# Key products of the second attention layer moved into the expert loop of the first

## The reference

```
# layer 0 mixture: 8 experts, two per token
scores = sigmoid(x @ gate_w.T);  _, sel = top_k(scores + expert_bias, 2)
top = scores at sel
for e in range(8):
    w = sum(where(sel == e, top, 0))
    out = out + square(relu((x * w) @ w_up[e].T)) @ w_down[e].T

# layer 1 attention: 16 heads of 64
q = x @ Wq;  k, v = split(context @ Wkv)
out = softmax(q k^T / 8) v @ Wout + bout
```

## Time and profile before

| | value |
|---|---|
| median of three runs | 838.61 us |
| the profiled execution, its own time | 840.57 us |
| span of the profiled execution | 839.2 us |
| mean granted TensorE clock | 0.952 |
| PE busy, share of the span | 721.9 us, 86% |
| DVE | 531.9 us, 63% |
| ACT | 502.9 us, 60% |
| POOL | 287.6 us, 34% |

### The profile page before, as it was taken

How to read it: one execution, slowest core, us unless ns; L and a number is a source line. 1 busy time by engine, 2 the same in 40 slices (tenths; PEclk the granted TensorE clock), 3 DMA queues, 4 the chain that set the end, 5 groups by cost and what they waited for, 6 DMA issues and landing times.

```text
span 839.2 us, 16594 instructions
## 1 busy us (share of the span) xinstructions
PE 721.9 (86%) x5129; PEld 596.4 (71%) x5129; DVE 531.9 (63%) x1847; ACT 502.9 (60%) x1688; POOL 287.6 (34%) x330
## 2 busy tenths in 40 slices
PE   3999895866787998999998989989999998877597
PEld 2667674656665877787985777878778876666597
DVE  3788674556657887754547888674242056986574
ACT  2988672445558987735556645666544248763375
POOL 1310311635543535532533534512010013343355
PEclk9999997689999999999999999999999999997699
DMA  8767974223226200002226730000000050000121
GB/s 268 281 200 247 307 207 144 88 74 84 74 66 230 76 2 14 14 17 69 62 83 193 201 120 1 2 1 1 0 1 1 1 201 1 1 14 21 52 72 47
DMA packets 37735, 74.21 MB, mean 88 GB/s; under 512 B 7360, under 2 KB 26944, under 8 KB 33680
## 3 DMA queue, kind: packets, MB, share of 16 engines
q1 hardware_dynamic: 32304, 62.97, 24.0%
q0 software_dynamic: 4768, 9.91, 3.5%
q10 hardware_dynamic: 576, 0.27, 0.1%
HBM read 63.03 MB, written 37.67 MB: 120 GB/s over the span
## 4 chain that ended last, share of the span: by engine, by line
PE 54%; DVE 18%; issue 10%; ACT 8%; POOL 5%; DMA 2%; another core or an unknown queue 1%; SPq 0%; POOLq 0%; DVEq 0%; ACTq 0%
PE bank L1143 10%; PE bank L1035 6%; PE bank L1105 5%; PE bank L996 5%; PE bank L1115 5%; PE bank L1011 4%; POOL out L2048 3%; DVE s_xn L1322 3%; PE bank L985 3%; PE bank L1095 2%; POOL xs_L L2041 2%; PE bank L940 2%; DVE s_total L1380 2%; ACT s_S L1838 2%; PE bank L1152 2%
## 5 line engine op out<-in xcount | busy, mean ns | idle before, releaser
L2013 POOL TENSOR_TENSOR s_S<-s_S,s_inv 128x462 f32<-128x462 f32 (+2 forms) x107 | 98.5, 936 | 134.9 <-DVE s_inv L1383 133.4
L1011 PEld LDWEIGHTS bank<-s_ident,s_S 128*128 128x128 f32 (+2 forms) x560 | 68.5, 144 | 56.7 <-issue 28.7
L996 PE MATMUL bank<-s_A,s_xTq 128*128 128x308 f32 (+1 forms) x256 | 99.4, 492 | 5.1 <-ACT s_S L1856 2.2
L1035 PE MATMUL bank<-s_VW,s_PT 128*128 128x128 f32 (+2 forms) x800 | 101.5, 283 | 2.4 <-DVE s_x L1410 2.4
L1011 PE MATMUL bank<-s_ident,s_S 128*128 128x128 f32 (+2 forms) x560 | 88.8, 283 | 16.2 <-ACT s_PT L1872 8.4
L1872 ACT ACTIVATE s_PT<-bank 128x512 f32<-128x512 f32 (+2 forms) x160 | 79.2, 517 | 34.8 <-PE bank L1011 22.1
L1035 PEld LDWEIGHTS bank<-s_VW,s_PT 128*128 128x128 f32 (+2 forms) x800 | 97.3, 199 | 3.3 <-DVE s_x L1410 2.9
L2041 POOL DMA_INDIRECT xs_L<-s_xn,s_sli x64 | 62.2, 972 | 105.2 <-DVE s_sli L1485 67.8
L1105 PE MATMUL bank<-s_xeT,s_hs 128*128 128x128 f32 x360 | 55.5, 295 | 13.7 <-ACT s_xeT L1894 13.4
L1914 ACT ACTIVATE s_hT<-bank,s_b1T 128x128 f32<-128x128 f32 x184 | 52.4, 370 | 21.5 <-PE bank L1115 9.6
L1838 ACT ACTIVATE s_S<-bank,s_peak 128x77 f32<-128x77 f32 x256 | 59.0, 374 | 7.6 <-DVE s_peak L1346 7.4
(11 more groups left out here) (234 smaller groups left out, 1621.8 us busy)
## 6 DMA issues: line engine op xcount, KB each, us to landing
xs_L<-xs_L SPq DMA_DIRECT2D x24, 1122.0 KB, 31.7
s_xe<-xs_L SPq DMA_DIRECT2D x85, 66.0 KB
s_moe<-in_L_w SPq DMA_DIRECT2D x2, 2048.0 KB, 18.3
s_moe<-in_L_w SPq DMA_DIRECT2D x8, 512.0 KB, 7.2
s_yb<-ys_L SPq DMA_DIRECT2D x12, 256.0 KB, 3.0
s_A<-in_keys SPq DMA_DIRECT2D x4, 616.0 KB, 6.5
s_arena<-in_L_w SPq DMA_DIRECT2D x2, 1024.0 KB, 12.0
s_arena<-in_L_h SPq DMA_DIRECT2D x2, 1024.0 KB, 9.3
```

What stands on the lines that cost most here:

```text
L996: w = mm(bank[j][:, 0:(g1 - g0) * KEYS], xTq_of(L, n)[:, i % 4, :], A[:, n, g0 * KEYS:g1 * KEYS], start=True, stop=True)
L1011: w = turn(bank[b][0:m, P * (t - t0):P * (t - t0) + P], S[s][:, P * t:P * t + m], ident)
L1035: w = mm(bank[b][:, 0:P], PT[k][0:m, t, :], VW[0:m, n, t, :], start=t == 0, stop=t == nt - 1)
L2013: p.tensor_tensor(val, val, rep(inv[s][:, h0:h1], KEYS, 2), ALU.mult).then_inc(normed.up(L, i, k), 1)
```

## The change

All pieces of the second layer's keys are taken out of the tail of `FIRST_LAYER`, and that tail is written anew: group 4's normalization stands before group 3's choice of experts, and group 4's gate product before group 3's placing. `experts` gets a table `among` of pieces put at the end of a step. For layer 0 it holds the products with their copies at steps 8 and 18, folds 0 to 3 at steps 11 to 14, folds 4 to 7 at 19 to 22, folds 8 to 13 at 27 to 32. Folds 14 and 15 stand at the head of `SECOND_LAYER`, around the up product of block 33.

```diff
@@ FIRST_LAYER, tail
-        send.0.10.1 ln.r.0.3.7 add.0.15 stat.0.15 half.1.1.0 prod.1.1.0 xt.r.0.3 route.0.3.0 ln.r.0.4.1 ln.r.0.4.2
...
+        send.0.10.1 ln.r.0.3.7 add.0.15 stat.0.15 xt.r.0.3 ln.r.0.4.1 ln.r.0.4.2 route.0.3.0
...
@@ SECOND_LAYER, head
-    back.0.0.0 X.0.34 U.0.33 H.0.32 D.0.31 X.0.35 U.0.34 H.0.33 D.0.32 X.0.36 U.0.35 H.0.34 D.0.33 X.0.37 U.0.36
+    fold.1.1.14 back.0.0.0 X.0.34 U.0.33 fold.1.1.15 H.0.32 D.0.31 X.0.35 U.0.34 H.0.33 D.0.32 X.0.36 U.0.35 H.0.34 D.0.33 X.0.37 U.0.36
@@ make_plan
-    def experts(L, last=None):
+    def experts(L, last=None, among={}):
...
                     if (what, s - d) == ("D", last):
                         return
+            layer(among.get(s, ""))
...
-    experts(0, 30)
+    experts(0, 30, {8: "half.1.1.0 prod.1.1.0 even.1.1.0", 18: "half.1.1.1 prod.1.1.1 even.1.1.1",
+                    **{t + h: f"fold.1.1.{h}" for t, h0 in ((11, 0), (15, 4), (19, 8), (19, 12))
+                       for h in range(h0, min(h0 + 4, 14))}})
```

More of the change, by code:

```diff
@@ L153 @@
         route.0.2.11 route.0.2.12 send.0.8.1 send.0.9.0 send.0.9.1 send.0.10.0 ln.r.0.3.4 ln.r.0.3.5 ln.r.0.3.6
-        send.0.10.1 ln.r.0.3.7 add.0.15 stat.0.15 half.1.1.0 prod.1.1.0 xt.r.0.3 route.0.3.0 ln.r.0.4.1 ln.r.0.4.2
[L155 to L163, removed]
+        send.0.10.1 ln.r.0.3.7 add.0.15 stat.0.15 xt.r.0.3 ln.r.0.4.1 ln.r.0.4.2 route.0.3.0
+        sigm.0.3 ln.r.0.4.3 ln.r.0.4.4 ln.r.0.4.5 ln.r.0.4.6 route.0.3.1 ln.r.0.4.7 route.0.3.2 route.0.3.3 xt.r.0.4
+        route.0.3.4 route.0.3.5 route.0.3.6 route.0.3.9 weigh.0.3.0 weigh.0.3.1 weigh.0.3.2 route.0.4.0 sigm.0.4
+        route.0.3.7 route.0.3.10 route.0.3.11 route.0.3.12 send.0.11.0 send.0.11.1 send.0.12.0 send.0.12.1
+        send.0.13.0 send.0.13.1 route.0.4.1 route.0.4.2 route.0.4.3 route.0.4.4 route.0.4.5 route.0.4.6 sched.0.0
+        route.0.4.9 weigh.0.4.0 weigh.0.4.1 weigh.0.4.2 route.0.4.10 route.0.4.11 route.0.4.12 send.0.14.0
+        send.0.14.1 load.L1v send.0.15.0 send.0.15.1 sched.0.1 sched.0.2 sched.0.3 sched.0.4 sched.0.5 sched.0.6
 """
 SECOND_LAYER = """
-    back.0.0.0 X.0.34 U.0.33 H.0.32 D.0.31 X.0.35 U.0.34 H.0.33 D.0.32 X.0.36 U.0.35 H.0.34 D.0.33 X.0.37 U.0.36
+    fold.1.1.14 back.0.0.0 X.0.34 U.0.33 fold.1.1.15 H.0.32 D.0.31 X.0.35 U.0.34 H.0.33 D.0.32 X.0.36 U.0.35 H.0.34 D.0.33 X.0.37 U.0.36
         H.0.35 D.0.34 X.0.38 U.0.37 H.0.36 D.0.35 U.0.38 H.0.37 D.0.36 H.0.38 D.0.37 D.0.38 half.1.0.0 prod.1.0.0
```

## The result

The changed kernel took 842.25 us (median of 17 runs, 837.88 to 844.77), the kernel before, on the same chip, 836.79 (17 runs, 834.62 to 840.24). The ratio on record is 1.0036, 95% interval 1.0021 to 1.0052: some 3.0 us slower, 1.8 to 4.4. The two medians lie further apart, 5.5 us, so the size is less certain than the sign. Forecast were 839.7 and no measurable change. The profiled execution of the changed kernel (838.9, span 837.5) is among the quicker of its 17 runs and that of the kernel before (840.57, span 839.2) lies above all 17 of its own, so I compare stretches and not spans.

What follows compares the result with a forecast made beforehand. The tail was taken as bound by group places and POOL's pitch, the loop by something serving blocks at 1.65 us. 840.57 - 1.8 + 2.9 = 841.7, in the runs' terms 838.61 + 1.1 = 839.7 us, range 834.5 to 849.5.

Steps and rivals of the forecast that it cites:

- its own test: Layer 0's expert loop: account wrong if first transpose to last down product changes by more than 4 us either way.
- The tail: Layer 0's routing tail: group 4's places come earlier, POOL sends ten times without a break, -1.8 us (-2.1 to 0).
- the 6.8 assumed: Tail, group 4's choice to places: 4.52 plus 2.26 for half of it doubling at 1.2 GHz; 1.1 us of slack.
- The 0.38: Tail: a row of group 4's normalization inside group 3's choice delays group 3's first send by 0.38 us.
- The tail does not get shorter: Rival, tail: group 4's places come at 166 as before, total 841.5 us; chance 0.13.
- The folds: Expert loop: 14 folds hidden by PE's stall, 0 us (at most 7.7); folds 14 and 15 behind it 0, at most 1.1.
- the stall comes on top: Rival, expert loop: stall comes every three blocks, folds and products add 12.4, total 849.2 us; chance 0.25.
- The stall breaks up: Rival, expert loop: inserted work disturbs an unlucky rhythm, loop 5.1 us shorter, total 831.7 us; chance 0.12.
- The products: Expert loop: each of two products holds PE and ACT 2.36 us; less time owed, +2.9 us for both.
- against it stands what is owed: Expert loop: time owed to a 1.65 us block server covers 0.92 us of each product on average.
- The clock: Tail and loop: PE at 1.2 GHz in the tail, full clock some 6 us after the loop starts; costed at 0.
- Something serves blocks at about 1.65 us each: Expert loop: blocks are served at about 1.65 us each whatever PE does; PE's stall is the time owed.

Runs made afterwards that it cites:

- run 3: Changed kernel with its emptied routing tail put back in the order of the kernel before, loop as changed: 813.64 us, ratio to before 0.9969.
- run 6: Kernel before with the second layer's key weights transferred ahead of eight clearing transfers: 809.73 us against 820.17, ratio 0.9872.
- run 2: Changed kernel with both products moved out of the loop to among the routing steps of groups 3 and 4, folds still in the loop: 815.26 us, ratio 0.9983.
- run 4: Changed kernel again, unaltered, on chip 3: 812.94 us, ratio to the kernel before 0.9959.
- run 10: Changed kernel with first product and folds 0 to 7 beside POOL's sends, second product at loop step 18, folds 8 to 13 at steps 19 to 32: 839.95 us against 838.23.
- run 11: Changed kernel with both products and folds 0 to 7 beside POOL's sends, folds 8 to 13 at loop steps 19 to 32: 839.12 us against 838.23.
- run 12: Changed kernel with key weights issued early, products among routing steps, folds 0 to 7 before the loop, 8 to 13 at steps 19 to 32: 839.22 us against 839.67.
- run 8: Changed kernel with both products and ten folds moved beside POOL's sends, four folds left in the loop, two behind it: 805.58 us, ratio to before 0.9823.
- run 5: Kernel before again, unaltered, on chip 12, for a second profile: 818.08 us in one execution.

## Why the prediction was right, and where it was not

The time came out in the forecast's range and sign, 2.5 us above it. That is less than the errors of its terms, some of which cancelled, so a good part of it is luck. By its own test the account of the loop was wrong: it was to change by no more than 4 us, and it changed by 4.6.

The tail. Right in mechanism (ten sends without a break), -2.8 measured for -1.8. The choice to the places of group 4 took 158.45 - 153.22 = 5.2, from 4.52, at a clock of 0.50 throughout, less than the 6.8 assumed; they were ready 2.2 before POOL needed them, not 1.1. The 0.38 for a row of group 4's normalization inside group 3's choice did not appear: group 3's first send came 9.24 after group 2's, where it had been 9.59, so that term was -0.35. And the first transpose followed the last send by 4.45 instead of 5.01, which I had left as it was. Runs 3 and 6 divide it: 1.6 to 1.8 for what is taken out (28.1 or 28.3 to 26.5) and 1.2 for the order. "The tail does not get shorter" is refuted.

What I could not see in the profile before is that the first product is bound by the landing of its weights. On the first chip that wait was covered by a stretch 17 us later (147.13 against 129.89 for group 2's first send) that is no property of the kernel. Uncovered, it adds 37.11 - 28.30 = 8.8 to the tail before, and the change then gains 37.11 - 25.32 = 11.8 there. That is why it makes the kernel faster on the quicker chips in spite of a loop that is 57.61 - 50.71 = 6.9 longer. The two make -4.9 and the timed runs -3.2; the profiles are single executions on two chips, and the wait itself varied from 8.62 to 11.00.

The folds. Costed at 0, near enough: a block with a fold takes 1.52, under the 1.65 of the first chip, and fourteen of them with two behind cost 1.6 in run 2. For the slower kind no run measures them alone. The rival "the stall comes on top" would have had the first chip's loop 12.4 longer, it became 4.6 longer. "The stall breaks up" would have made it 5.1 shorter, 59.7; it took 69.40.

The products. 2.36 each was right to 0.1 and to 0.3 in runs 4 and 2. The step that failed is "against it stands what is owed", 0.92 each: on the quicker kind, at a full clock, nothing was paid back. Without it the term is 2 x 2.36 = 4.7 beside the +4.6 measured on the first chip, but there the agreement is partly luck. The four blocks around its first product took 190.38 - 179.18 = 11.2, where four at 1.65 take 6.6, and the three around the second 207.88 - 198.79 = 9.1, where three take 5.0: 8.7 lost at the two, of which the rest of the loop made up 4.1. With the measured tail and loop alone the sum would be 836.79 - 2.8 + 4.6 = 838.6; what is missing to the measured +3.0 are the -2.6 ahead of the tail and the +3.6 behind the loop.

The clock. Costed at 0. In the tail it stood at 0.50 from 146 to 175 us, as forecast, and cost nothing that POOL's pitch did not cover. In the loop of the first chip it fell to 0.50 after each product, and the steps behind the first one take 188.31 - 186.39 = 1.92 for a bare block and 190.38 - 188.31 = 2.07 for one with a fold, instead of 1.02 and 1.52: 1.45 us together. The rule of the Trainium skill that the prediction cites ("TensorE: Matmul & The Clock Gate", "HAM oscillation — how this bites in real kernels") was placed at one spot only: the trace agrees with it in the tail, and also here, behind the product, where PE had stood 2.27; on chip 3, where it stood 0.97, the clock stays at 1.00. Run 4 loses 2.4 to 2.7 a product at the full clock; how much of the 4.6 is clock and how much the late copy no run separates.

The stall. "Something serves blocks at about 1.65 us each" holds on the slower kind only; on the quicker kind the bare loop goes at POOL's pitch of 1.26. On the slower kind the 4.94 of a group of three are three of POOL's pitches and one pause of 1.15. I took a property of a chip for one of the kernel.

Behind the loop, +3.6 against no forecast. On the slower kind, what is gained before 243 us was given back there in all five profiles: in runs 10 and 11 scores start 21.9 and 22.0 after the last down product, against 17.8 to 18.5 on the quicker kind (18.52 before and 19.34 in run 12 on the slower). The two kernels with a product in the loop are 0.35% slower, the two without one are even with before. That the product's interruption is what is left visible is argued from these four, not shown; the intervals of runs 10 and 11 overlap.

Open: why the slower chips are slow. From the start to the first send (92.6 and 92.4) and from the second layer's first scores to the end (580.6 and 580.7) the two profiles of the kernel before agree; all 22.4 us lie between. In that stretch signals arrive late, as in run 11, and waits end by a source that no row names. The -2.6 ahead of the tail belongs to it: from the first send to group 2's first it is 54.6 in the kernel before and in run 12, 52.0 to 52.7 in the changed kernel and runs 10 and 11, and 37.5 to 37.6 in all nine profiles of the quicker kind.

One pattern stands out: these waits end soon after POOL stops issuing indirect DMAs. The kernel before on the first chip, POOL and ACT:
```profile
130.15 0.96 POOL L2041 DMA_INDIRECT xs_L<-s_xn,s_sli  x1 [0.30 <-issue]
132.95 0.60 ACT L1872 ACTIVATE s_PT<-bank 128x512 f32<-128x512 f32 x1 [8.42 <-remote]
...
192.56 0.96 POOL L2048 DMA_INDIRECT ys_L<-s_yb,s_yi  x1 [0.31 <-issue]
194.37 0.28 ACT L1894 ACTIVATE s_xeT<-bank 128x128 f32<-128x128 f32 x1 [1.94 <-PE bank L1095]
```
130.15 is the last of eight sends in a row, 192.56 the last of three scatters. In all ten stalls of that loop over 1.9 ACT starts 0.75 to 0.92 after the last scatter of a burst has ended, and in the changed kernel ACT's wait of 4.94 ends 1.35 after POOL's last scatter (241.07 + 0.95). The same eight sends, 2.7 us after the first of them, on the first chip and then on chip 12, columns as in the earlier trace rows:
```profile
124.00:132.00 8.00, 2.32 (x10) 1.34 (x10) 0.00 (x0) 0.53 (x3) 5.58 (x6) 0.86 0.71 237
117.60:125.60 8.00, 7.23 (x128) 5.88 (x126) 5.67 (x21) 5.10 (x18) 5.56 (x6) 1.00 1.04 214
```
This is a coincidence in time, not a shown cause: on the quicker kind POOL scatters without a gap and ACT and DVE go on, and in the second layer on the first chip ACT is busy 6.67 of 8 us (316 to 324) beside four sends in a row. Whether it is in the transfers, in the semaphores or in something outside this core, nothing here tells.

## What to carry to other kernels

Ask of every moved instruction when its operands land, even if the trace shows no wait: a wait may be covered by lateness that another chip does not have. Put filler where the timeline shows an engine idle beside another's fixed pitch, here PE beside POOL's sends, and not into a pipeline that passes one bank and one copy engine from block to block: small pieces all but vanish there (0.12 each, run 2), a piece that needs the pipeline's banks costs its full length (2.4 to 2.7 each, run 4). And profile before and after on more than one chip before the sign of a change under 1% is believed.

## What the runs showed of the hardware

- Chips differ: the same program takes 816 to 820 us on three and 837 to 840 on two others and on the first one. Work placed beside the sends gave -1.8% on one kind (run 8) and +0.06% on the other (run 11).
- ACT saw PE's products 5.23 us after their start on one chip (run 11) and 2.12 on another (run 8), with the same instructions.
- Beside eight indirect DMAs in a row ACT was busy 0.53 of 8 us on the first chip and 5.10 of 8 on chip 12, in the same kernel (run 5).
- A 512 KB weight load queued behind eight clearing transfers landed 51.8 us after its issue, while its issue row shows 0.43 us (run 5).
- Indirect DMAs issued back to back start 1.26 us apart on POOL, on both kinds.
